# A pre-norm decoder layer on one core: the query-to-context vector summed on VectorE instead of by one-column products on TensorE

## What is computed

```
# c: normalised tokens [b, 112, 256]; q: context [b, 375, 256]
cq = einsum('bcd,bqd,d->bcq', c, q, w_cq) + b_cq
s = (c @ w_c + b_c)[:, :, None] + (q @ w_q + b_q)[:, None, :] + cq
a = softmax(s, axis=2)
c2q_att = einsum('bcq,bqd->bcd', a, q)
b_att = softmax(max(s, axis=2), axis=1)              # [b, 112]
q2c_att = einsum('bc,bcd->bd', b_att, c)[:, None, :] # [b, 1, 256]
x = concatenate([c, c2q_att, c * c2q_att, c * q2c_att], axis=-1)
z = x @ W_l.T + b_l
```

## Time and profile before

| | us |
|---|---|
| median of 3 runs | 758.57 (756.07 to 758.85) |
| time of the profiled execution | 759.8 |
| its span | 758.0 |
| TensorE busy, share of the span | 699.2, 92% |
| VectorE busy | 500.4, 66% |
| ScalarE busy | 408.3, 54% |
| GpSimd busy | 347.4, 46% |

### The profile page before, as it was taken

One profiled execution on the slowest core, in us unless ns is written; L12 is line 12 of the kernel. 1 busy time (PEld: TensorE's weight loads), 2 busy tenths in 40 slices (PEclk: granted clock), 3 DMA queues, 4 the chain that ended last, 5 costly groups with the idle time before them and its releaser, 6 DMA issues. The chain is left out here.

```text
span 758.0 us, 13311 instructions
## 1 busy us (share of the span) xinstructions
PE 699.2 (92%) x4496; PEld 616.8 (81%) x4496; DVE 500.4 (66%) x1232; ACT 408.3 (54%) x923; POOL 347.4 (46%) x482
## 2 busy tenths in 40 slices
PE   3879999999999999999999865989999999999997
PEld 2768888988988898889888854878888888888886
DVE  5686685775875866758758654766576667666442
ACT  4855766776776768567767532524243333333321
POOL 2756846765657558557575311323222223232222
PEclk9989999999999999999999998999999999999999
DMA  7622322313213313223001057022221203121200
GB/s 215 180 87 69 117 69 66 108 38 98 88 48 88 98 47 99 65 70 117 24 22 37 18 148 266 1 112 83 112 84 58 108 31 138 55 112 57 112 29 29
DMA packets 50769, 64.47 MB, mean 85 GB/s; under 512 B 3801, under 2 KB 49417, under 8 KB 49841
## 3 DMA queue, kind: packets, MB, share of 16 engines
q1 hardware_dynamic: 50736, 64.06, 26.7%
HBM read 56.60 MB, written 7.45 MB: 85 GB/s over the span
## 5 line engine op out<-in xcount | busy, mean ns | idle before, releaser
L1440 POOL TENSOR_TENSOR sg<-sg,cw_wide 128x512 f32<-128x512 f32 x56 | 74.6, 1331 | 187.9 <-ACT sg L1397 177.7
L1401 ACT ACTIVATE a_hi<-af 128x512 fp32r<-128x512 f32 x63 | 39.8, 632 | 157.4 <-DVE af L1521 157.4
L76 PE MATMUL bank<-h_hi,w_lo 128*128 128x512 f32 x224 | 92.6, 413 | 6.9 <-DVE w_lo L1538 5.1
L77 PE MATMUL bank<-h_lo,w_hi 128*128 128x512 f32 x224 | 90.5, 404 | 0.0
L78 PE MATMUL bank<-h_hi,w_hi 128*128 128x512 f32 x224 | 89.6, 400 | 0.0
L822 POOL TENSOR_TENSOR ctxt_lo<-ctxtf,ctxt_hi 128x375 fp32r<-128x375 f32 x64 | 58.4, 933 | 64.3 <-ACT ctx_hi L609 56.2
L1521 DVE TENSOR_TENSOR af<-bank,sg 128x512 f32<-128x512 f32 x63 | 43.2, 686 | 65.0 <-POOL sg L1440 61.9
L1526 DVE TENSOR_TENSOR a_lo<-af,a_hi 128x512 fp32r<-128x512 f32 x63 | 47.2, 749 | 34.9 <-ACT a_hi L1401 34.9
L827 POOL TENSOR_TENSOR ctx_lo<-ctxf,ctx_hi 125x256 fp32r<-125x256 f32 x96 | 68.9, 746 | 0.0
L76 PE MATMUL bank<-w_hi,a_lo 128*128 128x256 f32 x224 | 63.3, 283 | 0.0
L77 PE MATMUL bank<-w_lo,a_hi 128*128 128x256 f32 x224 | 63.2, 282 | 0.0
(11 more groups left out here) (252 smaller groups left out, 2293.3 us busy)
## 6 DMA issues: line engine op xcount, KB each, us to landing
cw_wide<-cw_scratch SPq DMA_DIRECT2D x7, 2048.0 KB, 7.1
ctxtf<-in_ctx_t SPq DMA_DIRECT2D x32, 375.0 KB
ctxf<-in_ctx SPq DMA_DIRECT2D x32, 375.0 KB
xt<-in_x SPq DMA_DIRECT2D x8, 448.0 KB, 3.7
x_scratch<-x2b SPq DMA_DIRECT2D x8, 448.0 KB, 3.2
x2n<-x_scratch SPq DMA_DIRECT2D x7, 512.0 KB, 4.7
x2t<-x_scratch SPq DMA_DIRECT2D x7, 512.0 KB, 3.9
out_dram<-x2t SPq DMA_DIRECT2D x7, 512.0 KB, 2.9
```

Of the source, the lines that this page charges most:

```text
L76: pe.matmul(dst, a_lo, b_hi, start=first, stop=False, **kw)
L77: pe.matmul(dst, a_hi, b_lo, start=False, stop=False, **kw)
L1401: act.activation(a_hi[n % (AHEAD + 1)][:, :], af[(p + n) % 2][:, :], ACT.Copy).then_inc(a_hi_ok, 1)
L1440: pool.tensor_tensor(sg[b][:, :], sg[b][:, :], cw_wide[p][:, ORDER[n], :], ALU.mult).then_inc(sgw_ok, 1)
```

## The change

The softmax rows are no longer transposed. Four fp32 products, with a column of the identity widened to [4, 128] as weights and the rows `mrow` [4, 112] as the moving operand, write each sequence's softmax row to all 128 partitions of `m_bank`. VectorE multiplies c transposed with them (two instructions, into the buffer of x4) and sums over the tokens (one reduction to q2c [128, 4, 2]). Then x4 is made as before. VectorE's wait for TensorE and all of this stand behind `h_low_pair(i + 1, 1)`. `v_product(0)` gets a wait for the q2c of the group before, since it overwrites the widened rows. Declarations of semaphores and of `b4` are left out here.

```diff
-            q2c = sb("q2c", [P, KB, G])
+            q2c = sb("q2c", [P, G, KB])
@@ TensorE, v_product(half)
+                        elif half == 0:
+                            pe.wait_ge(q2c_ok, i)
@@ TensorE, end of a group
                     turn_x(2)
-                    pe.transpose(m_bank[0:L, P:P + G], mrow[:, :], ident[0:G, 0:G]).then_inc(t_b, 1)
+                    for j in range(G):
+                        last = pe.matmul(m_bank[:, j * L:(j + 1) * L], ident[0:G, j:j + 1].to_broadcast([G, P]), mrow[:, :],
+                                         start=True, stop=True)
+                    last.then_inc(b_mm, 1)
                     turn_x(3)
                     z_c2q(0)
-                    pe.wait_ge(b4_ok, i + 1)
-                    for j in range(G):
-                        for k in range(KB):
-                            last = pe.matmul(m_bank[:, D + k * G + j:D + k * G + j + 1], c[:, j, k * P:(k + 1) * P], b4[:, j:j + 1],
-                                             start=True, stop=True)
-                    last.then_inc(q2c_mm, 1)
                     z_c2q(1)
@@ VectorE, end of a group
-                        if j == 0:
-                            dve.wait_ge(t_b, i + 1)
-                            dve.tensor_copy(b4[:, :], m_bank[0:L, P:P + G]).then_inc(b4_ok, 1)
-                    dve.wait_ge(q2c_mm, i + 1)
-                    dve.tensor_copy(q2c[:, :, :], m_bank[:, D:D + KB * G].rearrange("p (k g) -> p k g", k=KB)).then_inc(q2c_ok, 1)
                     if not last:
                         h_low_pair(i + 1, 1)
+                    dve.wait_ge(b_mm, i + 1)
+                    b_wide = m_bank[:, 0:TOK].rearrange("p (g t) -> p g t", g=G)
+                    for k in range(KB):
+                        w = dve.tensor_tensor(x4[:, :, k, :], ct[:, :, k, :], b_wide, ALU.mult)
+                    w.then_inc(cb_ok, 1)
+                    dve.wait_ge(cb_ok, i + 1)
+                    dve.reduce_sum(q2c[:, :, :], x4[:, :, :, :], AX).then_inc(q2c_ok, 1)
                     dve.wait_ge(q2c_ok, i + 1)
                     for k in range(KB):
-                        w = dve.tensor_tensor(x4[:, :, k, :], ct[:, :, k, :], q2c[:, k, :].unsqueeze(2).to_broadcast([P, G, L]), ALU.mult)
+                        w = dve.tensor_tensor(x4[:, :, k, :], ct[:, :, k, :], q2c[:, :, k].unsqueeze(2).to_broadcast([P, G, L]), ALU.mult)
                     w.then_inc(x4_ok, 1)
```

More of the change, by code:

```diff
@@ L243, in decoder_layer @@
             mexp, mrow = sb("mexp", [G, L]), sb("mrow", [G, L])
-            b4 = sb("b4", [L, G])
             shared_f = ctxf[:, 0, :, :].rearrange("p b d -> p (b d)")
             assert GU + D == NSB * D
-            q2c = sb("q2c", [P, KB, G])
+            q2c = sb("q2c", [P, G, KB])
             x4 = ctw
@@ L281, in decoder_layer @@
             t_m, mneg_ok, mexp_ok, minv_ok, mrow_ok = sem("m_transposed"), sem("m_max"), sem("m_exp"), sem("m_inv_sum"), sem("b_att_rows")
-            t_b, b4_ok, q2c_mm = sem("b_att_transposed"), sem("b_att_columns"), sem("q2c_product")
+            b_mm, cb_ok = sem("b_att_widened"), sem("c_times_b_att")
             q2c_ok, x4_ok, x4_hi_ok, x4_lo_ok = sem("q2c_ready"), sem("x4_ready"), sem("x4_hi_ready"), sem("x4_lo_ready")
```

## The result

The changed kernel takes 752.07 us (median of 6 runs, 746.36 to 753.16) where the kernel before takes 758.76 (6 runs, 756.07 to 761.75). The ratio is 0.9901, with an interval of 0.9876 to 0.9926: 7.5 us gained, 5.6 to 9.4. The two medians themselves lie 6.7 us apart. The forecast was 749.8 with a gain of 8.8. A second measurement on another chip gave 751.53 (5 runs) and a ratio of 0.9897 (0.9871 to 0.9924).

The account below looks back on a forecast made before the run. TensorE's list was taken to set the length. Group 0 -0.9, six groups -8.5 and the last group +0.6 sum to -8.8 us, from the median 758.57 to 749.8 us; range 746.5 to 755.5.

Parts of the forecast that it names:

- L571 costs 1.77 us a group: TensorE between z_c2q(0) and z_c2q(1): removing the 16 records of one-column products saves 1.77 us a group.
- The batch costs 0.90 us: TensorE: the four added fp32 products, eight records at the transposes' distance of 0.113 us, take 0.90 us.
- Rival (1): TensorE's added records cost 0.186 us each like the early fp32 product, 1.49 a batch; 754.3 us total; chance 0.12.
- rival (2): TensorE's added batch is cheap, 0.5 us or less, so the whole 1.77 shows; 746.5 us total; chance 0.08.
- rival (4): TensorE's fp32 weight loads do not overlap, 3.4 us a batch; slower, 770.1 us; chance 0.06 shared with another slower case.
- A wait of 0.40 us is filled: TensorE before z_c2q(0), groups 1 to 6: 0.40 us of added work fills the wait for VectorE's low part; 0.36 shows.
- VectorE's work is hidden in the loop: VectorE, groups 0 to 6: 2.2 us of added work fits into idle time with 0.4 us to spare.
- L1003 still waiting for ScalarE: Expected sign on VectorE: the instruction after x4 still waits for ScalarE, having had 2.67 us of idleness before.
- second margin: VectorE's x4 in the loop: ready 2.2 us before ScalarE reads it.
- The last group +0.6: Last group, no cover: x4 about 0.9 us later, z_q2c waits for GpSimd's low part, second block starts 0.6 us later.
- Group 0, -0.9: First group at granted clock 0.55: batch about 1.5 us, net gain 0.9 us (-1.77 + 0.87).
- (3): A mid-group wait on GpSimd or ScalarE takes back TensorE's gain; half the gain gives 754.2 us; chance 0.06.

## Why the prediction was right, step by step

**L571 costs 1.77 us a group: right.** 51.55 - 49.77 = 1.78 with everything removed. The reading was the distance from start to start between neighbours, less the usual step.

**The batch costs 0.90 us: mis-sized, it is 1.07.** The record's price of 0.113 was right to 0.001; the term lacks a fixed part of 0.17 us for each batch, which a distance within a row of equal records can't show. Rival (1), 0.186 a record, and rival (2), 0.5 a batch, are both out; so is rival (4): the weight loads overlap. The four passes of the Trainium skill (FP8 and Floating Point Precision, TensorE Precision Notes) would have made 0.75 us of it at 112 columns, by the forecast's estimate from that page. The 0.08 us that 96 fewer columns save show that columns hardly set the time here, so the estimate from columns does not describe these products.

**A wait of 0.40 us is filled: right in kind.** The bracket is gone, and moving the batch away from that place costs 0.75 us a group. So the exposed part of the batch was 0.51 against the kernel without it, and the net of a group -1.27 instead of -1.41.

**VectorE's work is hidden in the loop: right, by the wider of its two margins.** Multiplications 1.14 us (forecast 1.15) and reduction 1.09 (1.05):

```profile
L1146 DVE TENSOR_REDUCE q2c<-ctw x8: 1086/1086/1087, 78.7 to 429.5; 128x8 f32<-128x896 f32 x8
```

But "L1003 still waiting for ScalarE" was wrong: it has no wait left. h's low part did come when TensorE's order let it, and x4 took 0.8 us longer than its row had it, by a contention that was in no term. It did no harm, since the cover reaches to ScalarE's read of x4, which the forecast had as its second margin and the kernel with the work twice shows. The hand-overs of 0.05 us, for which the forecast had no row, took 0.03 and 0.04.

**The last group +0.6: it is +0.98.** The mis-sized term is the start of VectorE's chain, not the chain. The path in the trace of after, answering to the earlier trace rows:

```profile
428.28 1.14 DVE L1143 TENSOR_TENSOR ctw<-ct,bank 128x448 f32<-128x448 f32 x2
429.46 1.09 DVE L1146 TENSOR_REDUCE q2c<-ctw 128x8 f32<-128x896 f32 x1
430.58 1.16 DVE L1149 TENSOR_TENSOR ctw<-ct,q2c 128x448 f32<-128x448 f32 x2
431.66 1.38 DVE L164 TENSOR_SCALAR h<-x2n,mv,r 128x256 f32<-128x256 f32 x4
...
432.81 2.20 POOL L834 TENSOR_TENSOR cw_lo<-ctw,cw_hi 128x896 fp32r<-128x896 f32 x1 [7.60 <-ACT cw_hi L611]
...
435.06 0.37 PE L76 MATMUL bank<-wl_hi,cw_lo 128*112 128x256 f32 x1
```

`z_q2c` starts at 435.06, as soon as L834 is done at 435.01. This is the wait that was forecast, though the trace puts no bracket on it. From L1143 to the end of x4 it is 431.74 - 428.28 = 3.46 us, forecast 3.45. But the chain begins 8.08 us behind the transpose of the row maxima, where the forecast had 433.1 - 425.3 = 7.8: 0.3 us late, ahead of the added work. A stretch of low clock stands there:

```profile
426.00:430.00 4.00, 4.00 (x23) 3.89 (x23) 2.94 (x6) 0.94 (x2) 0.00 (x0) 0.58 0.00 0
```

What the clock took can be read from two siblings that have the same batch and a granted clock of 1.00 up to there. With VectorE's work twice the chain begins 423.22 - 415.31 = 7.91 us behind that transpose, and without the work at 421.56 - 413.64 = 7.92 (the rows are those of the work twice):

```profile
423.22 1.14 DVE L1144 TENSOR_TENSOR ctw<-ct,bank 128x448 f32<-128x448 f32 x2
...
420.00:424.00 4.00, 4.00 (x34) 3.75 (x34) 3.15 (x7) 2.06 (x4) 0.32 (x1) 1.00 0.02 4
```

So 0.11 of the late start is the batch and the delay that it passes on, and 0.17 the clock. Without the low clock the last group would cost about +0.8, an estimate from these rows; in the second trace of after, with more of it, the chain begins at 8.70.

**Group 0, -0.9: not seen.** The distance from 0 to 1 is 54.40 against 53.60, longer instead of shorter. In other kernels with the same batch in its place it is 50.97 to 54.32, so this group depends on when the clock falls and rises in an execution (in after it is 0.50 from 68.2 to 75.0, in before from 66.9 to 70.3), and a term of a few tenths can't be read from one trace.

**The sum.** By the profile pair: the four clean groups -5.1, the last distance -1.3, the group from 1 to 2 +0.3, group 0 +0.8, what is ahead of it +0.2, the last group +1.0: -4.1; and -2.6 in the second block, where nothing was edited. The -7.5 measured lies nearer to the forecast of -8.8 than the first block alone does. The clean terms as measured would be six groups at -1.27 and a last group at +0.8, -6.8, ahead of group 0 and of the clock in the loop. That the profiled before ran its second block at the long end explains most of the 2.6; whether the change has any hand in that block's length is open. So the total comes nearer to the forecast than the terms do, and that part is luck. The range, 746.5 to 755.5, holds both measurements' medians; of the rivals only (3) had a part in it, a loss elsewhere, and its place was the clock, not a wait.

## What to carry to other kernels

Price a short product by the distance of like records and add a fixed part for each batch of another form; then look for a wait of TensorE beside it, as one place further on the same batch cost 0.75 us more. Put work on an engine with room, but follow its results to the first reader that is on time, not to the next instruction: here 2.2 us, and even 4.4, were free in the groups of the loop and dear in the last. After a change that touches TensorE's order, compare the granted clock of many runs before and after; a gain can be paid back there without any instruction being added to the engine's list.

## What the runs showed of the hardware beyond this

**VectorE and GpSimd hold each other up.** L1149 reads two operands from SBUF. In the trace of before its 16 instances took 614 to 625 ns; after, where it comes later and meets GpSimd's L825 (count, ns min/median/max; then busy us and mean ns; then GpSimd ahead of and in the stretch of the rows of VectorE above):

```profile
L1149 DVE TENSOR_TENSOR ctw<-ct,q2c x16: 617/889/1160, 79.9 to 431.1; 128x448 f32<-128x448 f32 x16
...
L1149 DVE TENSOR_TENSOR ctw<-ct,q2c 128x448 f32<-128x448 f32 x16 | 14.9, 968 | 0.3
...
177.27 2.14 POOL L825 TENSOR_TENSOR ctx_lo<-ctxf,ctx_hi 125x256 fp32r<-125x256 f32 x3
...
182.32 2.91 POOL L825 TENSOR_TENSOR ctx_lo<-ctxf,ctx_hi 125x256 fp32r<-125x256 f32 x3
```

The mean is 968 instead of 617 ns and the longest 1160. GpSimd pays too: three L825 took 2.91 us there and 2.14 a little earlier. With VectorE's work twice, the same pair behind GpSimd's work took 1.20 us. The multiplication with one operand in PSUM (L1143, 1.14 us a pair) and the reduction (1086 to 1087 ns in all eight) were not held up in any row read. The Trainium skill, SBUF — State Buffer, section SBUF: two separate sides, describes the ports that VectorE and GpSimd share as an exclusive lock, taken by a VectorE instruction with two SBUF inputs against a GpSimd instruction that reads SBUF, in which the later one stands until the first is done. The rows of L1149 agree: one was longer by 543 ns, less than one L825. An instance of L164 was longer by 1.8 us beside one L834 of 2.11. L164 has only one input in SBUF; for such, the page names the modes in which VectorE uses two ports, and no run here shows whether it ran in one. By its length it went at no higher rate than L1149, 409 ns for 256 elements against 617 for 448, so the cause of this one stays open. The meeting of the two engines is worth a look in any change that moves such an instruction, even one that isn't edited.

**The clock can fall in a dense loop.** Before, no group of the loop was longer than another by more than 0.02 us; with four fp32 products of four rows in one place of it, one group or two held a stretch at a granted clock of 0.50 in six of eight executions traced, each beginning at the end of those products or within half a microsecond behind it (with the products made twice, during the second half of them). The mean clock separated the kernels more sharply than their times did: 0.979 against 0.984.
